# Side work of a fused attention kernel issued two parts at a time in every second quarter, and the products with the values one quarter earlier

## The chip, the cores and the metric

The kernel runs on one NeuronCore of a Trainium2 chip. The metric is the time of one execution on the device, in microseconds (us). The engines are named as in the profile: PE is TensorE (matmuls; PEld is its weight loads), DVE is VectorE, ACT is ScalarE, POOL is GpSimd, SP only issues transfers. Each engine works through its own list of instructions in order and waits at semaphores for the others.

## The reference

Eight batches of 1024 tokens and 256 channels go through four layers, each adding to x:

```python
x = x + attn_a(layernorm(x))   # one distance matrix for all 16 heads, causal softmax of -|p_i - p_j|/4
x = x + ffn(layernorm(x))      # r * (relu(xk W_k)^2 W_v), with xr, xk mixed from x and the token before
x = x + attn_b(layernorm(x))   # 16 heads of width 16, causal softmax, no output projection
x = x + ffn(layernorm(x))      # the same weights again
# attn_b, per batch and head:
scores = einsum('bhqd,bhkd->bhqk', q, k) / 4, causal
out    = einsum('bhqk,bhkd->bhqd', softmax(scores), v)
```

Everything is in float32; the queries and keys of attn_b are split into three bfloat16 parts each, so that one bfloat16 matmul with 96 rows gives the float32 scores.

## The kernel before

**The backbone.** attn_b sets the rhythm. Its work is cut into groups of 4 heads (4 groups for a batch, 32 in all), a group into 12 pieces, and a piece into 4 quarters, one for each head. Quarters are numbered u from 0 to 1535, then a few more to finish; quarters with negative numbers hold the work before attn_b can start. In this text q0 to q3 are the first to fourth quarter of a piece. In a quarter PE issues one matmul of the scores for the row maxima (L922, out `max_bank`, two buffers; it waits until DVE has reduced the one of two quarters before, L989 on the diagonal and L992 off it) and, 14 pieces behind it, one matmul of the transposed scores for the exponentials (L935, out `exp_bank`, two buffers; it waits for ACT's exponential L973 of two fills before). Key pieces narrower than 512 columns put 2 or 4 heads into one bank, and ACT then works only at the last of them. Once in a piece, after the two matmuls of q3, PE multiplies the exponentials of the piece before with the values: four float32 matmuls into `o_bank`, one for each head in a column group of its own (L954; the text calls these four "the products"). They wait for the last exponential of that piece, on the diagonal also for POOL's causal selection (L1011), and at the first piece of each half of the queries for ACT's copy of `o_bank` (L1059), which empties it from the half before and stands in ACT's list at q1 of the same piece.

**Side jobs.** All else on PE (the other three layers, the projections of attn_b, transposes) is cut into parts of some 0.4 to 0.9 us that are issued between the quarters. They write three `side` banks. `JOBS` and `stage_jobs` give each job the quarter in which its first part is due, its number of parts, the step between them and the delay after which another engine empties the bank. `place()` walks over the quarters and gives each quarter at most one part: the list is sorted by due time, the first of it is taken when it is due and, for a job's first part, when a bank is free. A part that comes late sets `shift`, which moves what the other engines have of that stage (through `WRITTEN_AT` and `clock`) by as many quarters; it is regained by one quarter in four. `maxima` (two transposes that carry the maxima of a group to a row, L1032) and `output` (L1066) are no parts: they are placed by themselves, `maxima` at q1 and `output` at q2, and come ahead of the parts of their quarter.

**Order.** `schedule` writes every engine's list with the same loop over the quarters: first the quarter's attention, then what is due of maxima, output and the stages. The job names that matter below: `tr` (transposes of the normalised x, L442, emptied by ACT L432), `values1` (values of attn_a, L615, needs both L432 copies), `keys` (L741, needs DVE's L675), `attend` (L633, needs ACT's L560 and POOL's L578), `project` and `values3` (L825, L841, for attn_b), `receptance` and `products` (L755, of the ffn).

A batch of attn_b is a turn of 192 quarters. By `place()` a steady turn holds 122 parts: 42 in its first 96 quarters and 80 in its last 96.

Of the kernel before, what the change touches and what calls it, by code (L numbers as in the profile page):

```python
# [18 lines left out]
GH = 4  # L19
# [32 lines left out]
def exp_before(e):  # L52

    return EXP_PER_GROUP * (e // len(PACK)) + sum(GH // heads for heads in PACK[:e % len(PACK)])
# [9 lines left out]
PIECES = B * NS  # L64
# [65 lines left out]
def stage_jobs(s, n, h):  # L130
    jobs = [((name, s, n, h, k), *when) for name, k, *when in JOBS["ln"]]
    body = "ffn" if s in ("ffn2", "ffn4") else s
    if body == "ffn" or h == 0:
        late = apart("att1", n) - APART["att1"]
        if s == "att1":
            work = [("values1", t, 16 + t + (TPH + late) * (t // TPH), 1, 1, 2) for t in range(NT)] + \
                [("positions", k, 29 + k + late * (k // 3), 1, 1, 1) for k in range(6)] + JOBS["attend"]
        else:
            work = JOBS.get(body) or [("project", j, project_at(n, j), 2, 1, 1) for j in range(8)] + \
            [("values3", j, project_at(n, 2 * j) + 2, 2, 3, 2) for j in range(4)]  # L140
        jobs += [((name, s, n, h, k), *when) for name, k, *when in work]
    return jobs


def place():

    parts, delay = [], {}
    for start, s, n, h in STAGES:
        for key, first, count, step, after in stage_jobs(s, n, h):
            delay[key] = after  # L150
            parts += [(start + first + step * k, key, k, k == count - 1) for k in range(count)]
    parts.sort(key=lambda part: part[0])
    rows = [(4 * NP * (g + 1) + 1, ("maxima", g)) for g in range(GROUPS)]
    rows += [(OUTPUT_AT[h] + 4 * NP * g + 5, ("output", g, h)) for g in range(GROUPS) for h in range(2)]
    rows += [(at, ("setup", k)) for k, at in enumerate(SETUP_AT)]
    rows.sort()
    quarters, bank, emptied, late = {}, {}, {}, []
    free, before, shift, u = [BEGIN, BEGIN, BEGIN], BEGIN, 0, BEGIN
    while parts or rows:
        while rows and rows[0][0] <= u and min(free) <= u:  # L160
            key = rows.pop(0)[1]
            k = free.index(min(free))
            quarters[key], bank[key], emptied[key] = [u], k, u + 2
            free[k] = u + 2
        if parts:
            at, key, k, last = parts[0]
            regained = max(0, shift - max(0, at - before) // 4)
            if at + regained <= u and (k > 0 or min(free) <= u):
                parts.pop(0)
                before, shift = at, max(regained, u - at)  # L170
                late.append((at, shift))
                if k == 0:
                    bank[key] = free.index(min(free))
                    free[bank[key]] = NEVER
                    quarters[key] = []
                quarters[key].append(u)
                if last:
                    emptied[key] = free[bank[key]] = u + delay[key]
        u += 1
    return quarters, bank, emptied, late  # L180


NEVER = 10 ** 6
BEGIN = STAGES[0][0]
PARTS_AT, BANK, EMPTIED_AT, LATE = place()
END = max(EMPTIED_AT.values()) + 20


WRITTEN_AT = {}
for k in range(BEGIN, END):  # L190
    since, shift = ([(BEGIN, 0)] + [entry for entry in LATE if entry[0] <= k])[-1]
# [11 lines left out]
def bass_hybrid(nc, x, wq, bq, wk, bk, wv, bv, wo, bo, w3d, b3d, wkqv, bkqv, w_r, w_k, w_v,  # L203
# [7 lines left out]
    with ExitStack() as ctx:  # L211
        def sb(name, shape, dt=F32):
            return ctx.enter_context(nc.sbuf_tensor(name, shape, dt))
# [37 lines left out]
        shift = sb("shift", [P, 2, TPH])  # L251
# [17 lines left out]
        parts = sb("parts", [P, 2, 3, HALF], BF16)  # L269
# [625 lines left out]
        emptied = [None, None, None]  # L895
# [14 lines left out]
        def pe_att3(u):  # L910
            pe = nc.tensor
            t, j = divmod(u, GH)
            e = t - LEAD
            if 0 <= t < PIECES:
                g, m = divmod(t, NP)
                if m == 0 and j == 0:
                    pe.wait_ge(stack_ready[g % STACKS], 16 * N_STACK_DMA * (g // STACKS + 1))
                tile, k0, k1 = QUERY_PIECES[m]
                r = g % STACKS
                if u >= MAX_BANKS:  # L920
                    pe.wait_ge(max_free, u + 1 - MAX_BANKS)
                pe.matmul(max_bank[u % MAX_BANKS][:, 0:k1 - k0], qs[r][0:KROWS, j, P * tile:P * (tile + 1)],  # L922
                          ks[r][0:KROWS, j, k0:k1], start=True, stop=True).then_inc(max_full, 1)
            if 0 <= e < PIECES:
                g, m = divmod(e, NP)
                if m == 0 and j == 0:
                    if g == 0:
                        pe.wait_ge(rows_of_ones, STACKS)
                    pe.wait_ge(crow_ready, 32 * (g + 1))
                kt, q0, q1 = KEY_PIECES[m]  # L930
                r = g % STACKS
                k, slot = exp_before(e) + j // PACK[m], j % PACK[m]
                if k >= EXP_BANKS and slot == 0:
                    pe.wait_ge(exp_done, k + 1 - EXP_BANKS)
                mm = pe.matmul(exp_bank[k % EXP_BANKS][:, (q1 - q0) * slot:(q1 - q0) * (slot + 1)],  # L935
                               ks[r][:, j, P * kt:P * (kt + 1)], qs[r][:, j, q0:q1], start=True, stop=True)
                if slot == PACK[m] - 1:
                    mm.then_inc(s_full, 1)
            if j == GH - 1 and 1 <= e <= PIECES:
                g, m = divmod(e - 1, NP)  # L940
                n = g // NG
                kt, q0, q1 = KEY_PIECES[m]
                h = 0 if m < TPH else 1
                if g == 0 and m == 0:
                    pe.wait_ge(consts_ready, 8)
                if g % NG == 0 and m == 0:
                    pe.wait_ge(v3_ready, 4 * n + 4)
                pe.wait_ge(exp_done, exp_before(e))
                if DIAGONAL[m]:
                    pe.wait_ge(sel_done, NT * g + NTH_DIAGONAL[m] + 1)  # L950
                if kt == 0:
                    pe.wait_ge(ot_ready, 2 * g + h)
                for j in range(GH):
                    mm = pe.matmul(o_bank[32 * j:32 * j + VW, q0 - HALF * h:q1 - HALF * h],  # L954
                                   v3[n % 2][:, kt, GH * (g % NG) + j, :], pt[:, (e - 1) % 2, j, 0:q1 - q0],
                                   start=(kt == 0), stop=(q1 - q0 == P), skip_group_check=True)
                mm.then_inc(pv_done, 1)
# [342 lines left out]
        @block.tensor  # L1300
        def _(pe):
            pe.wait_ge(consts_ready, 2)
            def stage(at, s, n, h):
                body = {"att1": [pe_att1(n), pe_positions(n)], "proj3": [pe_proj3(n), pe_values3(n)]}.get(s, []) if h == 0 else []
                return [pe_transposed(s, n, h)] + ([pe_ffn(s, n, h)] if s in ("ffn2", "ffn4") else body)

            schedule([pe_setup()], pe_att3, pe_maxima, pe_output, stage)
# [27 lines left out]
```

## Time and profile before

| | us |
|---|---|
| median of 3 runs | 2104.41 (2093.51 to 2106.41) |
| the profiled execution: its time | 2109.85 |
| its span, first to last instruction | 2108.1 |

| engine | busy us | share |
|---|---|---|
| PE | 1849.2 | 88% |
| DVE | 1467.0 | 70% |
| ACT | 1323.7 | 63% |
| POOL | 728.2 | 35% |

The mean granted clock of PE is 0.943 of full speed. A matmul's duration in the profile overlaps that of the next, so the time that a matmul really takes from PE is read from its start to the next one's start.

### The profile page before, as it was taken

How to read it: one execution, taken by the hardware profiler on the slowest of the kernel's cores; microseconds unless marked ns; L12 is line 12 of the kernel's file. 1: busy time of each engine (PE TensorE's matmuls, PEld its weight loads, DVE VectorE, ACT ScalarE, POOL GpSimd, SP SyncE). 2: the span in 40 equal slices, each digit the busy share in tenths (PEclk: the TensorE clock that was granted, in tenths of full speed). 3: DMA queues.
4: the chain of work that ended last, by engine and by line, in shares of the span. 5: the costliest groups of instructions: out<-in, count | busy, mean ns of one | idle time of the engine just before them, and what ended most of it. 6: DMA issues, size and time to landing. Idle time of an engine off the chain costs nothing. (4 is left out here: it accounts for less than half of the span.)

```text
span 2108.1 us, 32379 instructions
## 1 busy us (share of the span) xinstructions
PE 1849.2 (88%) x9842; PEld 922.5 (44%) x9842; DVE 1467.0 (70%) x4288; ACT 1323.7 (63%) x2585; POOL 728.2 (35%) x879
## 2 busy tenths in 40 slices
PE   5677898889997999889998899979998899988986
PEld 4453443335543455434543355434544345322423
DVE  5576778767676677667786667766776677768642
ACT  3564355876569565776758665695657766455664
POOL 1342332234333253333443243333532334312313
PEclk8797899999998999999999899989999999989998
DMA  3006113111131112410132111311124101322000
GB/s 85 1 23 123 26 56 67 31 31 32 55 76 31 31 31 82 80 21 12 41 110 42 31 31 56 76 31 31 34 83 76 22 11 41 99 33 50 13 21 20
DMA packets 64346, 97.26 MB, mean 46 GB/s; under 512 B 15655, under 2 KB 58029, under 8 KB 58030
## 3 DMA queue, kind: packets, MB, share of 16 engines
q1 hardware_dynamic: 64174, 95.20, 20.2%
q8 instruction: 80, 1.31, 0.3%
q14 instruction: 92, 0.75, 0.1%
HBM read 61.09 MB, written 33.55 MB: 45 GB/s over the span
## 5 line engine op out<-in xcount | busy, mean ns | idle before, releaser
L973 ACT ACTIVATE pt<-exp_bank 128x512 f32<-128x512 f32 (+1 forms) x1216 | 698.9, 582 | 526.6 <-PE exp_bank L935 521.0
L989 DVE CUSTOM_DVE_ANT_0 max_bank<-max_bank,mask 128x128 f32<-128x128 f32 (+3 forms) x1024 | 501.8, 500 | 400.9 <-PE max_bank L922 386.4
L922 PE MATMUL max_bank<-ks,qs 96*128 96x512 bf16 (+3 forms) x1536 | 523.5, 346 | 85.9 <-DVE piece_max L992 44.9
L935 PE MATMUL exp_bank<-qs,ks 98*128 98x512 bf16 (+3 forms) x1536 | 515.4, 342 | 40.0 <-ACT pt L973 37.0
L992 DVE TENSOR_REDUCE piece_max<-max_bank 128x1 f32<-128x512 f32 x512 | 344.1, 686 | 94.4 <-PE max_bank L922 90.2
L954 PE MATMUL o_bank<-pt,v 128*17 128x512 f32 (+3 forms) x3072 | 334.1, 508 | 13.7 <-POOL pt L1011 11.0
L922 PEld LDWEIGHTS max_bank<-ks,qs 96*128 96x128 bf16 x1536 | 150.9, 99 | 399.5 <-DVE piece_max L989 140.9
L1011 POOL TENSOR_SCALAR_AFFINE_SELECT pt<-pt 128x512 f32<-128x512 f32 x256 | 171.5, 670 | 412.6 <-ACT pt L973 411.8
L935 PEld LDWEIGHTS exp_bank<-qs,ks 98*128 98x128 bf16 x1536 | 152.4, 100 | 236.0 <-ACT pt L973 118.5
L633 PE MATMUL side<-vp,p 128*128 128x260 f32 x576 | 171.4, 423 | 28.7 <-ACT p L560 21.0
L412 ACT ACTIVATE xh<-xs,shift,rstd 128x256 f32<-128x256 f32 x256 | 149.7, 596 | 47.8 <-POOL shift L401 47.8
L589 POOL TENSOR_TENSOR sq<-sq 128x512 f32<-128x512 f32 (+1 forms) x96 | 97.3, 1013 | 226.3 <-ACT sq L536 226.3
L536 ACT ACTIVATE sq<-pb,neg_pos 128x512 f32<-128x512 f32 (+3 forms) x264 | 167.0, 633 | 3.6 <-ACT p L560 0.4
L741 PE MATMUL side<-pb,wkT 128*128 128x512 f32 x240 | 139.3, 669 | 9.3 <-DVE pb L675 9.2
L989 DVE DVE_READ_ACCUMULATOR2_ANT piece_max<- 128x1 f32 x1024 | 144.5, 141 | 0.3
L633 PEld LDWEIGHTS side<-vp,p 128*128 128x128 f32 x576 | 111.2, 207 | 74.1 <-issue 31.1
L825 PE MATMUL side<-xt,wkq 128*128 128x512 f32 x256 | 136.8, 619 | 3.0 <-ACT xt L432 1.5
L755 PE MATMUL side<-wrT,pb 128*128 128x256 f32 x480 | 126.3, 387 | 0.0
L755 PE MATMUL side<-wvT,pb 128*128 128x256 f32 x480 | 125.7, 386 | 0.0
L1090 POOL TENSOR_TENSOR xs<-xs,on 128x256 f32<-128x256 f32 x64 | 49.3, 770 | 208.5 <-DVE on L1080 208.4
L664 POOL TENSOR_TENSOR xs<-xs,tm 128x512 f32<-128x512 f32 x64 | 98.3, 1541 | 66.2 <-DVE tm L692 66.2
L791 POOL TENSOR_TENSOR parts<-x,parts 128x512 bf16<-128x512 f32 x64 | 74.9, 1170 | 108.3 <-DVE parts L775 108.3
(119 smaller groups left out, 2348.4 us busy)
## 6 DMA issues: line engine op xcount, KB each, us to landing
parts_dram<-parts SPq DMA_DIRECT2D x64, 384.0 KB, 2.6
qs<-parts_dram SPq DMA_DIRECT2D x192, 128.0 KB, 7.2
ks<-parts_dram SPq DMA_DIRECT2D x32, 384.0 KB, 4.7
xs<-in_L_attn_a_x_dram SPq DMA_DIRECT2D x16, 512.0 KB, 4.2
ks<-parts_dram SPq DMA_DIRECT2D x32, 256.0 KB, 5.4
out_dram<-xs SPq DMA_DIRECT2D x16, 512.0 KB, 3.1
ks<-parts_dram SPq DMA_DIRECT2D x32, 128.0 KB, 5.8
qs<-neg_maxT SPq DMA_DIRECT2D x64, 8.0 KB, 1.9
```

The source lines that it names most:

```text
L412: act.activation(xh[:, t, :], src[:, TPH * h + t, :], ACT.Identity, bias=shift[:, r, t:t + 1], scale=rstd[:, r, t:t + 1]).then_inc(xh_read ...
L536: mm = act.activation(sq[:, p % 2, c, 0:w], pb[:, c, q0:q1], ACT.Square, bias=neg_pos[:, kt, c:c + 1])
L633: mm = pe.matmul(bank[:, 0:VC], p1[:, at:at + P], vp[:, kt, :], start=(kt == 0), stop=(kt == t))
L741: mm = pe.matmul(bank[:, :], wkT[:, c, P * j:P * (j + 1)], xk[:, c, :], start=(c == 0), stop=(c == NC - 1))
L755: mm = pe.matmul(bank[:, C * t:C * (t + 1)], lhs[:, c, P * (2 * j + t):P * (2 * j + t + 1)], rhs[:, c, :], start=(c == 0), stop=(c == NC - 1))
L922: pe.matmul(max_bank[u % MAX_BANKS][:, 0:k1 - k0], qs[r][0:KROWS, j, P * tile:P * (tile + 1)], ks[r][0:KROWS, j, k0:k1], start=True, stop= ...
L935: mm = pe.matmul(exp_bank[k % EXP_BANKS][:, (q1 - q0) * slot:(q1 - q0) * (slot + 1)], ks[r][:, j, P * kt:P * (kt + 1)], qs[r][:, j, q0:q1] ...
L954: mm = pe.matmul(o_bank[32 * j:32 * j + VW, q0 - HALF * h:q1 - HALF * h], v3[n % 2][:, kt, GH * (g % NG) + j, :], pt[:, (e - 1) % 2, j, 0: ...
L973: act.activation(pt[:, e % 2, j + 1 - heads:j + 1, 0:w], exp_bank[k % EXP_BANKS][:, 0:heads * w].rearrange("p (j n) -> p j n", j=heads), A ...
L989: dve.tensor_tensor_reduce(scores, scores, mask[:, HALF - w:HALF], 1.0, LOWEST, ALU.add, ALU.max, piece_max[:, j, m:m + 1]).then_inc(max_f ...
L992: dve.tensor_reduce(piece_max[:, j, m:m + 1], scores, AX.X, ALU.max).then_inc(max_free, 1)
L1011: pool.affine_select(out=block, in_=block, compare_op=ALU.is_ge, fill=0.0, base=0, pattern=[[0, GH], [1, P]], channel_multiplier=-1).then_ ...
```

## The change

`place()` gives a quarter with u of 0 or more no part when u is even and up to two when u is odd. In exchange a part may be taken ahead of its due time: a job's first part by one quarter, its other parts by two. Below u = 0 all stays as it was. The products with the values are issued at q2 instead of q3, with the same waits. Nothing is added to or taken from what is computed; `maxima`, `output`, L1059 and the selections keep their places.

```diff
-        if parts:
+
+        for _ in range(1 if u < 0 else 2 * (u % 2)):
+            if not parts:
+                break
             at, key, k, last = parts[0]
             regained = max(0, shift - max(0, at - before) // 4)
-            if at + regained <= u and (k > 0 or min(free) <= u):
-                parts.pop(0)
-                before, shift = at, max(regained, u - at)
-                ...
+            if at + regained > u + (u >= 0) * (1 if k == 0 else 2) or k == 0 and min(free) > u:
+                break
+            parts.pop(0)
+            before, shift = at, max(regained, u - at)
+            ...
...
-            if j == GH - 1 and 1 <= e <= PIECES:
+            if j == GH - 2 and 1 <= e <= PIECES:
                 g, m = divmod(e - 1, NP)
```

## Rows read from the trace of the kernel before

**Rows 1.** The page, part 1: an engine's busy time, share, instructions.
```profile
PE 1849.2 (88%) x9842; PEld 922.5 (44%) x9842; DVE 1467.0 (70%) x4288; ACT 1323.7 (63%) x2585; POOL 728.2 (35%) x879
```
**Rows 2.** Stretches: length, busy us and instructions of each engine, granted clock, DMA.
```profile
1125.20:1242.00 116.80, 101.84 (x553) 47.04 (x550) 80.78 (x245) 86.14 (x177) 41.66 (x56) 0.93 0.16 28
1242.00:1371.00 129.00, 123.29 (x680) 66.25 (x678) 96.38 (x285) 78.78 (x151) 49.00 (x53) 1.00 0.28 67
...
1137.00:1151.00 14.00, 11.34 (x74) 5.22 (x75) 11.95 (x30) 12.16 (x26) 5.80 (x7) 1.00 0.41 59
1151.00:1171.00 20.00, 15.58 (x81) 4.01 (x73) 12.32 (x35) 19.29 (x38) 5.39 (x6) 0.91 0.00 1
...
1206.00:1214.00 8.00, 7.39 (x29) 1.99 (x28) 7.07 (x17) 4.45 (x8) 1.82 (x3) 0.57 0.00 0
1214.00:1242.00 28.00, 28.00 (x147) 14.70 (x146) 18.14 (x56) 19.84 (x39) 12.23 (x13) 1.00 0.00 1
```
**Rows 3.** Timeline of PE, 80-part half: start, duration, line, tiles, idle before.
```profile
1007.72 0.33 PE L922 MATMUL max_bank<-ks,qs 96*128 96x384 bf16 x1
1007.88 0.38 PE L935 MATMUL exp_bank<-qs,ks 98*128 98x512 bf16 x1
1008.10 1.03 PE L755 MATMUL side<-wvT,pb 128*128 128x256 f32 x4
1008.96 0.33 PE L922 MATMUL max_bank<-ks,qs 96*128 96x384 bf16 x1
```
**Rows 4.** Waits of PE, whole span: us in total, times, longest.
```profile
PE max_bank L922 <- DVE piece_max L992: 44.9, 80, 1.4
PE exp_bank L935 <- ACT pt L973: 37.0, 90, 0.6
PE max_bank L922 <- DVE piece_max L989: 35.1, 89, 1.3
...
PE side L633 <- ACT p L560: 21.0, 11, 8.1
PE o_bank L954 <- POOL pt L1011: 11.0, 16, 1.2
...
PE side L1032 <- DVE neg_max L1001: 8.5, 14, 0.8
```
**Rows 5.** Timeline around a copy of o_bank, where ACT is full.
```profile
1157.80 0.62 ACT L1059 ACTIVATE ot<-o_bank 128x512 f32<-128x512 f32 x1
...
1157.98 0.39 PE L935 MATMUL exp_bank<-qs,ks 98*128 98x512 bf16 x1 [0.49 <-ACT pt L973]
```
**Rows 6.** Timeline around a maxima job, 80-part half.
```profile
1304.77 0.38 PE L922 MATMUL max_bank<-ks,qs 96*128 96x512 bf16 x1
...
1305.25 1.05 PE L954 MATMUL o_bank<-pt,v 128*17 128x512 f32 x8
1306.23 1.12 PE L825 MATMUL side<-xt,wkq 128*128 128x512 f32 x2
...
1308.49 0.28 PE L1032 MATMUL side<-identb,neg_max 128*32 128x128 bf16 x2
```
**Rows 7.** Timeline around the first values1, 80-part half.
```profile
1339.79 0.39 PE L922 MATMUL max_bank<-ks,qs 96*128 96x512 bf16 x1
1339.82 0.59 ACT L432 ACTIVATE xt<-side 128x512 f32<-128x512 f32 x1
...
1340.46 1.14 PE L615 MATMUL side<-wvp,xt 128*128 128x259 f32 x4
```
**Rows 8.** Timeline around the first keys of a layer.
```profile
1209.05 0.74 DVE L675 SCALAR_TENSOR_TENSOR pb<-pb,cols,xt 128x512 f32<-128x512 f32 x1
...
1209.19 0.61 PE L922 MATMUL max_bank<-ks,qs 96*128 96x512 bf16 x1 [0.23 <-DVE piece_max L992]
```
**Rows 9.** Timeline: the first attend of a batch.
```profile
1130.35 0.68 PE L633 MATMUL side<-vp,p 128*128 128x260 f32 x2 [1.30 <-ACT p L560]
```
**Rows 10.** Waits of PE in the 80-part half, 1242 to 1371 us.
```profile
PE side L600 <- DVE on L1080: 0.8, 1, 0.8
PE side L841 <- ACT xt L432: 0.8, 1, 0.8
PE side L1032 <- DVE neg_max L1001: 0.8, 1, 0.8
PE side L442 <- ACT x L784: 0.6, 1, 0.6
```

More of the change, by code:

```diff
@@ L164, in place @@
             free[k] = u + 2
-        if parts:
+        for _ in range(1 if u < 0 else 2 * (u % 2)):
+            if not parts:
+                break
             at, key, k, last = parts[0]
             regained = max(0, shift - max(0, at - before) // 4)
-            if at + regained <= u and (k > 0 or min(free) <= u):
-                parts.pop(0)
-                before, shift = at, max(regained, u - at)
[L171 to L178, printed above, removed]
+            if at + regained > u + (u >= 0) * (1 if k == 0 else 2) or k == 0 and min(free) > u:
+                break
+            parts.pop(0)
+            before, shift = at, max(regained, u - at)
+            late.append((at, shift))
+            if k == 0:
+                bank[key] = free.index(min(free))
+                free[bank[key]] = NEVER
+                quarters[key] = []
+            quarters[key].append(u)
+            if last:
+                emptied[key] = free[bank[key]] = u + delay[key]
         u += 1
```

## Prediction

> **What bounds the kernel now.** I first read the engines' shares: PE is busy 88% of the span, the next, DVE, 70% [rows 1]. A share is a mean over unlike stages, so I read stretches next. Steady turns repeat, and I take the one from 1125.2 to 1371 us. Its half with 80 parts takes 129.0 us with PE busy 123.29; the half with 42 takes 116.8 with PE busy 101.84 [rows 2]. Inside the first kind PE has no gap at all (28.00 of 28.00 us from 1214 on); inside the second ACT alone is full for 20 us (19.29), and before it DVE and ACT share the blame (11.95 and 12.16 of 14) [rows 2]. So the bound alternates.
>
> The timeline of a full quarter shows what PE is made of: 0.16 us for 384 columns of maxima, 0.22 for 512 of exponentials, 0.86 for a part, each start following the last at once [rows 3]. The product of 512 columns takes 0.98 (1305.25 to 1306.23) [rows 6]. Going over from one kind to another costs nothing, so **doing two parts in a row saves PE no time by itself**: a gain can only be a wait that goes.
>
> The waits of PE say how much there is: 44.9 + 35.1 us for DVE to free a maxima bank, 37.0 for ACT to free an exponentials bank, 21.0 at attend, 11.0 at products for a selection, 8.5 at maxima [rows 4]. These are understated: a 512-column record lasts 0.38 us where its successor can start after 0.22, so each of the 259 bank waits hides 0.16 more. Bank waits are thus 117 + 41 = 158 us.
>
> **Evenness.** With 512-column banks and parts of 0.86 everywhere, q0 to q3 take 1.30, 1.30, 1.30 and 2.28 us before, and 0.44, 2.16, 1.42 and 2.16 after; the piece takes 6.18 both times. A bank wait depends on the time over two quarters, since banks are reused after two. Before, these windows are 2.60, 2.60, 3.58, 3.58; after, 2.60, 3.58, 3.58, 2.60: the same four, rotated. So where PE is full I expect no bank wait to come or go. Where no parts are, moving the products only rotates the piece. A gain needs pieces with a few parts, half bound by PE in q3 and by DVE in q0 to q2; there the longest quarter (products and part) is split.
>
> **The parts, by hand from the rule.** Due times in the ffn stages come in even-odd pairs (keys at 842 and 843, then 844 and 845). After, both parts of a pair go into the odd quarter before (841, 843). Attends likewise (784, 785 into 783). The projections of a turn, which now slip until the next stage is 4 quarters late, fit without lateness: values1, due at 932, goes from 936 to 933, and attn_a behind it starts 4 quarters sooner. Parts issued per turn stay 122. Five terms follow, then the sum.
>
> 1. **Products one quarter sooner: +14 us.** Of the 384, the 63 behind a copy of `o_bank` are the tight ones. The copy stands at q1; it starts 0.2 us before the last scores matmul of q3 in a full ACT, and lasts 0.62 [rows 5]. At q2 PE comes after 0.44 us of matmuls, where ACT needs an exponential and the copy, about 0.6 + 0.6 less overlap: some 0.5 us too early, 32 us for 63. Where two parts stand in q1 they cover it (1.72), and where ACT or DVE is full PE would have waited at the next bank anyway. Selections on the diagonal already cost 11.0 [rows 4]; one quarter less slack at narrow pieces adds a few more. Bounds 0 and 38; I take 14, as two thirds lie in the stretches bound by ACT or DVE.
>
> 2. **Maxima: +8.** L1032 needs DVE's reduction of the last scores of the group, issued in q3 (1304.77), and is reached at q1, 3.6 us later, with the 0.98 of the products between [rows 6]. After, the products stand ahead of that q3, so PE arrives up to 0.98 sooner at a place where it already waits. 31 x 0.98 = 30 is the upper bound, 0 the lower (all absorbed by DVE, which works on meanwhile). Worked through group by group with the parts in between it is 15; half of the groups are in DVE-bound stretches: 8.
>
> 3. **Parts pulled ahead: +19.** Tight ones per turn: values1 starts 0.05 us after ACT's second L432 ends (1340.41), and one quarter earlier PE would be there at 1339.79: 0.7 us of waiting, twice [rows 7]; by the new plan L432 and values1 even share a quarter. Keys: L675 ends at 1209.79, PE would be there at 1209.19: 0.7 [rows 8]. With small ones about 3 us a turn, in stretches where PE is the bound, so nothing hides it: 6.5 turns give 19. Bounds 0 and 30. The ffn's products and receptance have over 4 us of slack and cost nothing.
>
> 4. **Less lateness: -25.** The first attend waits 1.30 us [rows 9], the second about as much, because regaining `shift` squeezes the chain from squares to selection; without lateness each has a quarter more. Of 21.0 us [rows 4], 8.1 of it ahead of u = 0, I take 13 as gained. ACT's squares start 4 quarters sooner, out of the ACT-full stretch and into one where ACT is busy 78.78 of 129 [rows 2]: 1 us a turn, 6. Waits for `side` banks and the like (0.8 each [rows 10]) are dealt anew; a quarter of some 4 us a turn, 6. Bounds 0 and 50.
>
> 5. **Bank waits in mixed pieces: -22.** Of the 158 us most lie in stretches where ACT or DVE is full, which no order mends. Limiting each piece with parts to what DVE and ACT both had idle leaves 44 us. I take half; bounds 0 and 60.
>
> Sum: 14 + 8 + 19 - 25 - 22 = -6 us on the profiled execution's 2109.85, so 2104. The median lies 5.4 below that execution, so I say 2098. A measurement of this kernel can tell about 1% from no change.
>
> **A clock rule.** Around 1206 to 1214 the granted clock is 0.57 of full, so most of it is at 1.2 GHz; the stretch from 1214 on, full of work, has 1.00, that is 2.4 GHz [rows 2]. Ahead of 1206 PE had kept waiting for DVE. The Trainium skill ("TensorE: Matmul & The Clock Gate", Part 1) says the throttled state is the default and sustained activity lifts it. By that rule, new waits that thin out PE's work could start a further slow stretch; the trace agrees that slow stretches follow waiting. This is rival D.
>
> **Rivals.**
> A, likeliest (0.40): gains and costs nearly cancel, 2098; own range 2078 to 2130.
> B (0.32): smoothing works better. Terms 4 and 5 near their far ends (-50, -45) against costs of 41 give 54 less: 2050. For it: the bank waits are the largest item [rows 4] and the bound alternates within pieces. Against: windows over two quarters are the same four, and ACT is full in 20 us of each turn.
> C (0.18), the other side: the cover of the pulled parts and the products is gone. Costs 30 + 20 + 28 against 38 of gain give +40: 2145. It decides if values1, keys and the first products of each half wait over 0.7 us each in the 80-part half. For it: they start within 0.1 us of their inputs now [rows 7, 8].
> D (0.10): the clock. The half with 42 parts has a mean of 0.93 [rows 2], so 16 us of it at half speed. As much again would cost 8 us a turn, some 48 in all: 2146. Less of it would gain as much.
>
> **How the numbers follow.** Faster by over 1% (below 2083): B 0.32 and 0.03 of A and D: 0.35. Slower by over 1% (above 2125): C 0.16, D 0.07, 0.03 of A: 0.26. Between: 0.39. B ends at 2050 and C at 2145; 2052 to 2140 leaves out about 2 in 10.
>
> **What the profile after would show.** Right: bank waits (117 in rows 4) near 90, attends (21.0) near 12, products waiting 20 to 30 instead of 13.6, L1032 near 15 instead of 8.5, values1 and keys together near 15; the 80-part half 128 to 131 us, the other 112 to 117. B: the 42-part half below 112. C: the 80-part half above 132 with waits at L615, L741 and L954. D: granted clock away from 0.943. The forecast fails if bank waits rise in the 80-part half (windows misjudged), or if pairing makes `side` banks short.

## The result, and the profile after

The change makes the kernel **slower by 9.1%**: 2294.28 us (median of 4 runs, 2287.51 to 2301.20) against 2104.41 for the kernel before (median of 3 runs; a fourth one, 2414.66 us, was disturbed and is left out), ratio 1.0911 [1.0860, 1.0963]. The ratios here and below are estimates from repeated runs with a 95% interval, and can differ a little from a quotient of two medians. The profiled execution took 2301.20 us with a span of 2299.4, so 191.3 us more than the span of before. The four lines that the diff adds to `place()` move every later line of the kernel by 4: L922 of before is L926 here, L442 is L446, L741 is L745, L954 is L958.

The shares of the kernel after, the page's part 1:

```profile
PE 1929.3 (84%) x9842; PEld 934.0 (41%) x9842; DVE 1477.4 (64%) x4288; ACT 1328.3 (58%) x2585; POOL 712.3 (31%) x879
```

Beside [rows 1] the counts are the same and DVE, ACT and POOL are busy nearly as long. PE is busy 80 us longer with the same matmuls, and idle 111 us longer. The first points to its clock: the mean granted clock fell from 0.943 to 0.907. The traces record only two levels, full and half (2.4 and 1.2 GHz), so (1 - clock) x 2 x span is the time at the lower one: 240 us before, 428 after.

The same steady turn as in [rows 2] (stretch, length, busy us and instructions of each engine, granted clock, DMA):

```profile
1220.40:1346.00 125.60, 105.55 (x550) 47.14 (x548) 81.03 (x244) 85.15 (x175) 40.31 (x54) 0.89 0.15 26
1346.00:1490.00 144.00, 127.32 (x678) 66.99 (x677) 97.20 (x283) 80.62 (x153) 48.05 (x54) 0.96 0.24 60
```

The half with 42 parts went from 116.8 us to 125.6, the half with 80 from 129.0 to 144.0. The half in which PE had been almost gapless lost most, and its clock is no longer full throughout (0.96).

The waits of PE over the span (total us, times, longest), to be read against [rows 4]:

```profile
PE side L446 <- ACT xh L416: 61.9, 44, 9.7
PE max_bank L926 <- DVE piece_max L996: 38.1, 86, 1.3
PE side L745 <- DVE pb L679: 37.8, 29, 3.6
PE max_bank L926 <- DVE piece_max L993: 37.5, 100, 1.3
PE exp_bank L939 <- ACT pt L977: 28.9, 64, 0.9
PE side L1036 <- DVE neg_max L1005: 25.9, 25, 1.6
PE o_bank L958 <- ACT ot L1063: 18.9, 31, 1.1
PE o_bank L958 <- POOL pt L1015: 17.4, 20, 1.7
PE side L637 <- ACT p L564: 12.8, 3, 8.1
PE side L619 <- ACT xt L436: 11.5, 7, 1.8
```

The same lines of before that [rows 4] did not need:

```profile
PE side L442 <- ACT xh L412: 22.8, 7, 9.7
...
PE side L741 <- DVE pb L675: 9.2, 3, 3.6
...
PE side L615 <- ACT xt L432: 2.6, 6, 0.8
PE o_bank L954 <- ACT ot L1059: 2.6, 14, 0.2
```

Two jobs that hardly waited before, the transposes of the normalised x and the keys, now head the list: 7 waits became 44, and 3 became 29.

**Where the 191 us went.** Records of matmuls overlap and hide short waits, so PE's whole timeline is taken from start to start, and what each step costs at full clock is subtracted (0.22 us for 512 bfloat16 columns, 0.86 for a part, as in [rows 3]). In the stretches that the trace records at the lower level the same columns take twice as long: all 110 steps of the trace of before that lie within a side part and wholly in such a stretch take about twice their time at full clock, or more. So for a step in such a stretch its cost at full clock is counted once more, as the price of the clock. What is left stands at the line ahead of which it falls. The work at full clock is 1600 us in both kernels (and in every variant below but one). The rest, in us:

| beyond the work | before | after | difference | products one quarter earlier alone | pairs alone |
|---|---|---|---|---|---|
| lower clock | 89.7 | 162.8 | +73.1 | 158.8 | 92.4 |
| `tr` (L442) | 36.9 | 81.5 | +44.6 | 41.5 | 83.6 |
| `keys` (L741) | 21.4 | 53.8 | +32.4 | 21.1 | 56.1 |
| the products (L954) | 52.1 | 78.3 | +26.2 | 105.1 | 52.4 |
| `maxima` (L1032) | 12.4 | 30.6 | +18.2 | 28.2 | 17.8 |
| `values1` (L615) | 13.8 | 25.7 | +11.9 | 22.4 | 25.1 |
| scores for the maxima (L922) | 126.9 | 132.0 | +5.1 | 131.9 | 130.5 |
| L825, L600, L841 together | 26.4 | 30.0 | +3.6 | 26.1 | 30.5 |
| scores for the exponentials (L935) | 62.5 | 52.6 | -9.9 | 39.1 | 65.5 |
| `attend` (L633) | 36.9 | 26.2 | -10.7 | 35.8 | 33.4 |

These differences add up to +194.5 and the lines not listed to -3.1, so nothing of the 191.3 is missing. The last two columns are kernels of the first experiments. The lower clock is the largest single item. A rough check needs no account: in the stretches at the lower level PE is busy 191.8 of 244.3 us before and 360.4 of 431.6 after, and about half of that busy time is what the lower level adds. Of the +73.1 us, 69 stand in steps that no idle time of PE follows, so they are not hidden in a wait. In the fourteen traces of this case a microsecond at the lower level costs 0.34 to 0.38 us; below I take 0.37. At the banks the listed waits fall from 117.0 us to 104.5, and by this account, which counts hidden ones too, L922 and L935 together go from 189.4 to 184.6: no real change.

### The profile page after: what moved, and what is told of

Read it like the earlier page. It is cut to its first block and busy times, and to the rows that moved or that the text cites. A ratio compares the mean times of both kernels' runs of the same rounds, so it can differ in the third digit from the quotient of the medians.

```text
span 2299.4 us, 32379 instructions
## 1 busy us (share of the span) xinstructions
PE 1929.3 (84%) x9842; PEld 934.0 (41%) x9842; DVE 1477.4 (64%) x4288; ACT 1328.3 (58%) x2585; POOL 712.3 (31%) x879
## 3 DMA queue, kind: packets, MB, share of 16 engines
q1 hardware_dynamic: 64174, 95.20, 18.4%
## 5 line engine op out<-in xcount | busy, mean ns | idle before, releaser
L977 ACT ACTIVATE pt<-exp_bank 128x512 f32<-128x512 f32 (+1 forms) x1216 | 689.9, 577 | 678.6 <-PE exp_bank L939 676.6
L926 PE MATMUL max_bank<-ks,qs 96*128 96x512 bf16 (+3 forms) x1536 | 538.2, 356 | 82.6 <-DVE piece_max L996 38.1
L939 PE MATMUL exp_bank<-qs,ks 98*128 98x512 bf16 (+3 forms) x1536 | 535.9, 356 | 32.8 <-ACT pt L977 28.9
L958 PE MATMUL o_bank<-pt,v 128*17 128x512 f32 (+3 forms) x3072 | 357.5, 540 | 36.7 <-ACT ot L1063 18.9
L926 PEld LDWEIGHTS max_bank<-ks,qs 96*128 96x128 bf16 x1536 | 153.7, 100 | 491.8 <-DVE piece_max L993 207.0
L637 PE MATMUL side<-vp,p 128*128 128x260 f32 x576 | 159.5, 414 | 20.7 <-ACT p L564 12.8
L745 PE MATMUL side<-pb,wkT 128*128 128x512 f32 x240 | 143.4, 730 | 37.9 <-DVE pb L679 37.8
L446 PE MATMUL side<-ident,xh 128*128 128x128 f32 x512 | 82.1, 287 | 69.3 <-ACT xh L416 61.9
L637 PEld LDWEIGHTS side<-vp,p 128*128 128x128 f32 x576 | 113.3, 205 | 51.9 <-issue 18.2
L958 PEld LDWEIGHTS o_bank<-pt,v 128*17 128x17 f32 x3072 | 54.1, 97 | 169.4 <-issue 106.6
L759 PE MATMUL side<-wvT,pb 128*128 128x256 f32 x480 | 114.5, 382 | 0.0
L759 PE MATMUL side<-wrT,pb 128*128 128x256 f32 x480 | 113.9, 380 | 0.0
```

The costliest lines, as they stand in the source:

```text
L637: mm = pe.matmul(bank[:, 0:VC], p1[:, at:at + P], vp[:, kt, :], start=(kt == 0), stop=(kt == t))
L745: mm = pe.matmul(bank[:, :], wkT[:, c, P * j:P * (j + 1)], xk[:, c, :], start=(c == 0), stop=(c == NC - 1))
L759: mm = pe.matmul(bank[:, C * t:C * (t + 1)], lhs[:, c, P * (2 * j + t):P * (2 * j + t + 1)], rhs[:, c, :], start=(c == 0), stop=(c == NC - 1))
L977: act.activation(pt[:, e % 2, j + 1 - heads:j + 1, 0:w], exp_bank[k % EXP_BANKS][:, 0:heads * w].rearrange("p (j n) -> p j n", j=heads), A ...
```

## The experiments

Twelve kernels ran, each beside runs of the kernel before on its own chip. That kernel's median differs by chip (2107.79 for the first four, 2088.36 for the next four, 2093.14 for the last four), so kernels of different groups are compared by their ratios, not by their microseconds. "Time at the lower clock" is (1 - clock) x 2 x span. It too differs by chip for the kernel before (240, 196 and 205 us), so the last column gives what a kernel has above the before of its own chip, medians of runs; the column ahead of it is the profiled execution. Lines of a kernel that carries the new `place()` have the numbers of the kernel after (in shifted and repaired one more), of others those of before.

| kernel | ratio to before | lower clock, us | above before, us |
|---|---|---|---|
| pv_only | 1.0579 [1.0528, 1.0630] | 435 | +173 |
| pairs_only | 1.0515 [1.0483, 1.0547] | 257 | +10 |
| ahead_only | 1.0132 [1.0103, 1.0162] | 247 | +1 |
| tight_later | 1.0638 [1.0596, 1.0680] | 399 | +152 |
| pairs_even | 1.0249 [1.0215, 1.0283] | 273 | +84 |
| two_due | 1.0023 [1.0003, 1.0044] | 193 | -3 |
| pv_copy | 1.0526 [1.0487, 1.0565] | 352 | +151 |
| pv_busy | 1.0791 [1.0750, 1.0832] | 271 | +67 |
| shifted | 1.0697 [1.0654, 1.0741] | 385 | +182 |
| repaired | 1.0466 [1.0429, 1.0504] | 328 | +134 |
| pv_fixed | 1.0416 [1.0379, 1.0454] | 331 | +120 |
| maxima_q2 | 1.0053 [1.0028, 1.0077] | 214 | +30 |

### One half of the change at a time

**pv_only**: the kernel before with only the products moved.

```diff
-            if j == GH - 1 and 1 <= e <= PIECES:
+            if j == GH - 2 and 1 <= e <= PIECES:
```

> The kernel before with only the products moved from q3 to q2 (parts one a quarter, as before). Theory S (side parts lost the time they had behind their inputs): little changes at the side jobs; the waits at the products (13.6 us before, 36 after) and at maxima (8.5 before, 25.9 after) rise as in the whole change, so 2105 + 25 = about 2130, and granted clock near 0.94. Theory P (the products moved ahead are the cause): most of the 189 us is here, over 2230. Theory G (it balances the quarter, as the forecast had it): 2085 to 2105.

**pairs_only**: the kernel after with the products back at q3 (`j == GH - 1`).

> The kernel before with only the new placing of the parts (two by two in odd quarters, ahead of their due time), the products still at q3. Theory S: most of the loss, 2105 + 150 = about 2250, with PE waiting over 50 us at the transposes L446 for ACT and over 30 at keys L745 for DVE, as in the whole change. Odd quarters at q3 now hold products and two parts, so q3 is the longest quarter by far; bank waits at q1 and q2 rise a little. Theory P: within 1% of before. The two kernels pv_only and pairs_only should then add up to about the whole, +189.

Measured: 2234.18 and 2215.43 us beside 2107.79. Each half is slow by itself, and 5.8% + 5.2% is more than the 9.1% of both; that the products alone would cost 25 us was wrong. They are slow in different ways. The two waits in pairs_only:

```profile
PE side L446 <- ACT xh L416: 62.3, 45, 9.7
...
PE side L745 <- DVE pb L679: 37.6, 29, 3.6
```

So these two waits come from the pairs alone, to within half a microsecond. In pv_only:

```profile
PE max_bank L922 <- DVE piece_max L992: 39.7, 84, 1.4
PE o_bank L954 <- POOL pt L1011: 37.0, 27, 2.1
PE max_bank L922 <- DVE piece_max L989: 35.3, 99, 1.3
PE o_bank L954 <- ACT ot L1059: 24.0, 42, 1.1
PE side L1032 <- DVE neg_max L1001: 23.5, 26, 1.6
```

The products wait 61.0 us where they waited 13.6 (11.0 and 2.6), `maxima` 23.5 instead of 8.5, the waits for a maxima bank, the next on the way, hardly shrink (80.0 to 75.0), and the lower clock holds for 435 us instead of 240: 69 of the 132 us by the table above. The halves of the steady turn in pv_only show where:

```profile
1181.70:1306.60 124.90, 107.92 (x550) 48.63 (x548) 80.82 (x245) 86.55 (x177) 40.76 (x55) 0.86 0.15 26
1306.60:1441.40 134.80, 122.98 (x679) 65.98 (x677) 97.10 (x282) 79.18 (x151) 49.80 (x54) 1.00 0.26 64
```

The half with few parts has a clock of 0.86 instead of 0.93 and 8.1 us more; the other keeps its clock and has 5.8 us more, all of it waits.

### Pulling ahead or pairing?

The pairs do two things: parts are taken ahead of their due time, and even quarters are left empty. **ahead_only** does the first alone, one part a quarter as before; **two_due** allows two in a quarter but none ahead, which takes the lateness away and leaves the rest; **pairs_even** puts the pairs into the even quarters. All have the products at q3.

```diff
 # ahead_only
-        for _ in range(1 if u < 0 else 2 * (u % 2)):
+        for _ in range(1):
 # two_due
-        for _ in range(1 if u < 0 else 2 * (u % 2)):
+        for _ in range(1 if u < 0 else 2):
-            if at + regained > u + (u >= 0) * (1 if k == 0 else 2) or k == 0 and min(free) > u:
+            if at + regained > u + 0 or k == 0 and min(free) > u:
 # pairs_even
-        for _ in range(1 if u < 0 else 2 * (u % 2)):
+        for _ in range(1 if u < 0 else 2 * (1 - u % 2)):
```

> The kernel before, one part in every quarter and the products at q3, but a part may be taken ahead of its due time as in the change (first part by one quarter, others by two). Separates the pulling ahead from the empty even quarters. If the pulling ahead alone costs (a part reaches its input one quarter sooner), the transposes, keys and values1 wait as in the whole change and it takes over 2180. If it is the empty even quarter between input and part (0.44 us instead of 1.3) that takes the slack, this one loses only what the forecast's third term said, some 20 to 40 us: 2125 to 2145.

> The kernel before, but a quarter may take two parts when both are due, none ahead of its time; no part is late any more in the steady turns. Tests the gain from less lateness that the forecast's fourth term took (25 us for the whole change). By that term 2105 - 20 = about 2085; if lateness cost nothing, 2105; if values1 and keys then wait for inputs because the time was needed, 2110 to 2120.

> The mirror of the change: two parts in every even quarter (q0, q2), none in odd ones, with the same pulling ahead, and the products at q3 as before. The balance over the quarters is that of the change, but the tight parts (transposes, keys, values1), all due in even quarters, stand where they are due, and a loaded quarter lies between their input and them. Theory S (the parts lost the time behind their inputs): waits at L446 and L745 go back to 38 and 10 to 25 us and the products wait as before, so 2095 to 2130. Theory E (two parts in one quarter cost in themselves, whatever they wait for): it stays near pairs_only, 2190 to 2230.

Pulling ahead costs 1.3%, some 28 us. The other three quarters of the pairs' 5.2% come with the empty even quarters. In ahead_only the keys already wait as often as in the kernel after, the transposes much less:

```profile
PE side L446 <- ACT xh L416: 29.9, 14, 9.7
PE side L745 <- DVE pb L679: 29.6, 30, 3.6
```

With the pairs in the even quarters both waits are nearly those of before, though just as many quarters are empty:

```profile
PE max_bank L926 <- DVE piece_max L993: 51.4, 128, 1.3
PE max_bank L926 <- DVE piece_max L996: 48.4, 83, 1.8
...
PE side L446 <- ACT xh L416: 24.6, 8, 9.7
...
PE side L745 <- DVE pb L679: 11.1, 10, 3.6
```

So the pairing and the empty quarters by themselves don't make them wait. By `place()` the first transposes of one stage, for example, stand at quarter 830 before, at 829 in the kernel after and at 830 in pairs_even; the first keys at 842, 841 and 842. In the even phase nothing that is due in an even quarter is pulled ahead. The long waits need both: a part that is pulled by one quarter (ahead_only: 14 waits of `tr`) and an empty quarter ahead of it (44). What pairs_even still loses (2.5%, some 52 us) is to a good half the lower clock: it holds for 84 us more than in the before of the same chip, by estimate 31 us of time (84 x 0.37). The rest stands at the bank waits, 127.6 us for the three instead of 117.0, and in many small ones. two_due is no faster than before (1.0023), although the attends' 21.0 us are down to 12.2: **taking the lateness away alone is worth nothing that can be measured.**

### Are the two waits the cause?

**tight_later** gives the two jobs their quarter back: due one quarter later in the kernel after. They are then due in odd quarters and are not pulled: by `place()` the first transposes stand at 831 (830 before, 829 after), the first keys at 843 (842 and 841). **shifted** begins every stage one quarter later, with the same effect on all jobs.

```diff
 # tight_later
-JOBS = {"ln": [("tr", c, 12 + c, 1, 1, 2) for c in range(NC)],
+JOBS = {"ln": [("tr", c, 13 + c, 1, 1, 2) for c in range(NC)],
-        "ffn": [("keys", j, 24 + 2 * j, 2, 1, 1) for j in range(2)] +
+        "ffn": [("keys", j, 25 + 2 * j, 2, 1, 1) for j in range(2)] +
 # shifted
+STAGES = [(start + (start >= 0), s, n, h) for start, s, n, h in STAGES]
```

> The whole change, but the transposes are due one quarter later and so are the keys, which by the rule of placing puts them two quarters later where they had been pulled ahead. Theory S: the waits at L446 (61.9 us) and at keys L745 (37.8) fall by more than half, and the time by 60 to 100 us, to about 2210. Theory C (the slow clock is the cause and not a consequence): the waits fall but cold time stays near 430 us and the time stays above 2260.

> The whole change with every side stage that starts at u = 0 or later begun one quarter later. Balance over the quarters as in the change (pairs in q1 and q3, products at q2), but the tight parts are now due in odd quarters and are no longer taken ahead, and their inputs' quarter is a loaded one. Theory S: waits at L446 (61.9) and L745 (37.8) return to about 23 and 17, the time to 2294 - 80 = about 2210, near pv_only (the waits at products, selections and maxima stay). Theory E (two parts in one quarter cost in themselves): it stays over 2270.

Both take the waits away, and the time follows in part: the ratio falls from 1.0911 to 1.0638 and 1.0697, some 57 and 45 us. In shifted the two waits are 22.7 us (7 times) and 8.2 (3 times), as before. In tight_later:

```profile
PE side L446 <- ACT xh L416: 19.4, 4, 9.7
...
PE side L745 <- DVE pb L679: 7.1, 3, 3.6
```

By the start-to-start account `tr` falls from 81.5 to 31.9 and `keys` from 53.8 to 8.4, 95 us in all. Later waits take back a part: L922 132.0 to 160.7, products 78.3 to 86.7, `values1` 25.7 to 32.3; the lower clock gives another 9 (162.8 to 153.5). A wait of PE taken away here is worth a little more than half its length. So the two waits are a cause of the loss, but hardly of the low clock: tight_later still has 152 us more of it than its before.

### What the products wait for

**pv_copy** is pv_only with ACT's copy of `o_bank` one quarter earlier as well (q0); to keep the order of the rest, `output` and the last ffn stage start stay where they were. **pv_fixed** has `maxima` one quarter later (q2) on top. **maxima_q2** is the kernel before with `maxima` at q2.

```diff
 # pv_copy, pv_fixed (against before, beside GH - 2)
-OUTPUT_AT = [4 * (LEAD + TPH + 1) + 1, 4 * (LEAD + NP + 1) + 1]
+OUTPUT_AT = [4 * (LEAD + TPH + 1), 4 * (LEAD + NP + 1)]
 # pv_fixed, maxima_q2
-    rows = [(4 * NP * (g + 1) + 1, ("maxima", g)) for g in range(GROUPS)]
+    rows = [(4 * NP * (g + 1) + 2, ("maxima", g)) for g in range(GROUPS)]
```

> pv_only (products at q2) with ACT's copy of o_bank one quarter earlier as well (q0 instead of q1), the output transposes staying at q2. If the products' loss comes from the copy standing one quarter ahead of them, the wait for L1059 (24 us in pv_only) vanishes and the time falls by 20 to 40 us, to about 2200; the waits for the selection (37 us) and at maxima (23.5) stay. If the copy only hides other waits, the time stays at 2230.

> pv_copy with maxima one quarter later (q2, behind the products). Expected: the 23 us that PE waits there go, 2198 - 20 = about 2175, that is +70 on before; the rest is the selection (36 us) and half clock (353 us of it). If the wait only moves on to the bank waits: no change.

> The kernel before with nothing changed but maxima one quarter later (q2 instead of q1). PE waits 8.5 us at this place before, 14 times, and its DMA has quarters to spare; so 2105 - 5 to 10, a ratio of 0.995 to 1.0. If the DMA of the maxima row is late then, PE waits at L935 for qs<-neg_maxT instead.

In pv_only the wait for the copy looks like this (timeline: start, duration, engine, line, tiles, idle before):

```profile
1198.63 0.60 ACT L1059 ACTIVATE ot<-o_bank 128x512 f32<-128x512 f32 x1
...
1199.38 1.05 PE L954 MATMUL o_bank<-pt,v 128*17 128x512 f32 x8 [0.82 <-ACT ot L1059]
```

With the copy at q0 this wait goes from 24.0 us to 0.2. The ratio goes from 1.0579 to 1.0526; the two intervals overlap, so it isn't shown that the time fell at all. By the start-to-start account the products lose 27.6 us less (105.1 to 77.5) and the bank waits take 13.9 back (171.0 to 184.9). With `maxima` later too it is 1.0416, which is 1.1% below pv_copy and outside the intervals. The same move of `maxima` in the kernel before does nothing good (1.0053), although it clears L1032's 8.5 us: the lower clock holds for 30 us more than in the before of its chip, by estimate 11 us, which is the whole loss, and the waits of L935 for the DMA of the maxima row, named in the expectation, are 5.7 us instead of 0.8.

What pv_fixed keeps above before, 4.2%, has three parts that the profile shows: products waiting for selections, waits for a maxima bank (100.9 us instead of 80.0), and the clock, with 120 us more at the lower level by estimate 44 of the 87 us. The first:

```profile
PE o_bank L954 <- POOL pt L1011: 38.7, 33, 2.1
```

Its chain in pv_only, where it is longest:

```profile
1247.98 0.28 DVE L468 SCALAR_TENSOR_TENSOR sq<-sq 128x128 f32<-128x128 f32 x1
...
1248.30 0.31 ACT L550 ACTIVATE sq<-sq 128x128 f32<-128x128 f32 x1 [3.36 <-DVE sq L468]
1248.52 0.58 ACT L973 ACTIVATE pt<-exp_bank 128x512 f32<-128x512 f32 x1
...
1249.26 0.67 POOL L1011 TENSOR_SCALAR_AFFINE_SELECT pt<-pt 128x512 f32<-128x512 f32 x1 [3.86 <-ACT pt L973]
1250.07 0.63 PE L954 MATMUL o_bank<-pt,v 128*17 128x256 f32 x8 [2.06 <-POOL pt L1011]
```

The exponential that the selection needs stands in ACT's list behind an instruction of the other attention, L550, which waits 3.36 us for DVE. Its counterpart before has the same chain, of which the products at q3 hid one quarter:

```profile
1189.36 0.63 PE L954 MATMUL o_bank<-pt,v 128*17 128x256 f32 x8 [0.97 <-POOL pt L1011]
```

0.97 us became 2.06: at such narrow pieces a quarter is one part and two short matmuls, 1.1 us, and all of it is lost.

### What the clock does

**pv_busy** asks whether the low clock is a cause or only an effect. It is pv_only with the scores for the maxima issued twice (into the same bank, same values) in the 680 quarters that have no part, so that PE is busier where it is thin; 117 us of work more at full clock.

```diff
+IDLE = set(range(PIECES * 4)) - {u for at in PARTS_AT.values() for u in at}
-                pe.matmul(max_bank[...], ..., start=True, stop=True).then_inc(max_full, 1)
+                for _ in range(2 if u in IDLE else 1):
+                    mm = pe.matmul(max_bank[...], ..., start=True, stop=True)
+                mm.then_inc(max_full, 1)
```

> pv_only with the scores matmul of the maxima issued twice in the 680 quarters that hold no side part (the same result into the same bank), which keeps PE busier where it would wait. Theory C (slow clock is a cause of its own): time at half clock falls from 435 us to under 250 and the kernel gets faster, 2234 - 30 = about 2200, although 680 x 0.2 = 136 us of work is added. Theory W (the clock only follows the waits and costs little): the time stays or rises by 20 to 80 us.

Measured: 1.0791 against pv_only's 1.0579, so 117 us of work cost 2.1%, some 45 us. Above the before of its own chip the lower clock holds for 67 us instead of pv_only's 173, by estimate 39 us of time; the rest of the added work, some 30 us, went into waits that were there anyway (all items of the account but the clock: 470.8 to 427.8 us). So the clock falls because PE's work is thinner, and it costs time of its own; but filling up does not pay for itself. The time came out as theory W had it, the clock more as theory C.

### A version with all repairs

**repaired** is the kernel after with every stage one quarter later (shifted), the copy at q0 and `maxima` at q2.

> shifted, with the copy of o_bank a quarter earlier (q0, output transposes still at q2) and maxima a quarter later (q2). If the loss is the sum of the slacks taken (parts behind inputs, copy, maxima), what is left over is the selection wait and the clock: 2150 to 2170. If a part of the loss is none of these, it stays above 2190.

It takes 2191.91 us beside 2093.14, 1.0466: half of the loss is back, but it isn't faster than before, so by the expectation's own sign a part of the loss is none of the slacks named. Its steady turn and its waits:

```profile
1162.30:1288.00 125.70, 106.01 (x548) 48.36 (x547) 82.17 (x245) 87.63 (x179) 41.34 (x55) 0.89 0.15 26
1288.00:1418.00 130.00, 121.27 (x680) 65.95 (x678) 95.87 (x282) 77.51 (x149) 47.90 (x53) 1.00 0.26 66
```

```profile
PE max_bank L927 <- DVE piece_max L994: 63.4, 123, 2.3
PE max_bank L927 <- DVE piece_max L997: 57.6, 120, 1.7
```

The 80-part half is almost that of before (130.0 against 129.0) with a full clock. The 42-part half stays at 125.7 us against 116.8, and the waits for a maxima bank are 121.0 us instead of 80.0. The lower clock holds for 134 us more than in the before of the same chip, by estimate 50 of the 98 us that are left. Why the banks are the worse for products at q2 and paired parts in pieces with few of them, while DVE has 35% of that half to spare, is not known; no run tells it apart.

No kernel of the study beats the one before.

## Why the prediction was wrong

The forecast was -6 us on the profiled execution, the result +191. Set against the start-to-start table the miss of 197 us divides among its steps so (the lines not listed take 3 back):

| step | said | measured, in the whole change | missed |
|---|---|---|---|
| 3, parts pulled ahead | +19 | +44.6 +32.4 +11.9, and 12.3 at L825 and L600: +101.2 | 82 |
| clock (rival D, not in the sum) | 0 | +73.1 | 73 |
| 5, bank waits | -22 | +5.1 -9.9: -4.8 | 17 |
| 1, products | +14 | +26.2 | 12 |
| 2, maxima | +8 | +18.2 | 10 |
| 4, less lateness | -25 | -10.7 at attends, -8.7 at L841: -19.4 | 6 |

Two steps failed above all: term 3, and the clock, which the sum put at nothing.

**Term 3 failed in its kind, not only in its size.** It took the timeline of before and asked when PE would be there one quarter sooner. But in that timeline the even quarter before a consumer holds a part of its own; in the new order it holds none. Look at the transposes, before:

```profile
1216.22 0.60 ACT L412 ACTIVATE xh<-xs,shift,rstd 128x256 f32<-128x256 f32 x1
1216.29 1.02 PE L741 MATMUL side<-pb,wkT 128*128 128x512 f32 x2
...
1217.37 0.38 PE L935 MATMUL exp_bank<-qs,ks 98*128 98x512 bf16 x1
1217.59 0.60 PE L442 MATMUL side<-ident,xh 128*128 128x128 f32 x4
```

and after:

```profile
1316.91 0.38 PE L926 MATMUL max_bank<-ks,qs 96*128 96x512 bf16 x1
1317.13 0.38 PE L939 MATMUL exp_bank<-qs,ks 98*128 98x512 bf16 x1
...
1318.14 0.60 ACT L416 ACTIVATE xh<-xs,shift,rstd 128x256 f32<-128x256 f32 x1
...
1318.79 0.65 PE L446 MATMUL side<-ident,xh 128*128 128x128 f32 x4 [1.28 <-ACT xh L416]
```

Before, ACT is done at 1216.82 and PE arrives at 1217.59, a slack of 0.77 us that a look at waits alone doesn't show. After, PE is free at 1317.35 and starts at 1318.79: 1.44 us of waiting. The slack fell by 0.77 + 1.44 = 2.21 us, which is a quarter pulled, 1.30, and the part that is gone from the even quarter, 0.86. By the first alone it would wait 0.53, and the prediction did not even list this job among the tight ones. pairs_even and tight_later show the cause: where the parts aren't pulled, by the other phase or by due times one later, 44 and 29 waits are 8 and 10, or 4 and 3. The price that term 3 put on pulling alone was near in size, 19 said, 28 measured by ahead_only, but not in its make-up: the keys alone rise by 27 us there (21.4 to 48.7), the rest nearly cancels.

For the keys the prediction had the place and the row [rows 8] but 0.7 us each (the row gives 0.60); in the kernel after, the first keys of a layer wait longer, and their two parts (x4) then run at the lower clock, 3.78 us where the next two take 1.88 at full clock:

```profile
1308.93 0.74 DVE L679 SCALAR_TENSOR_TENSOR pb<-pb,cols,xt 128x512 f32<-128x512 f32 x1
1309.73 3.78 PE L745 MATMUL side<-pb,wkT 128*128 128x512 f32 x4 [0.89 <-DVE pb L679]
...
1314.76 1.88 PE L745 MATMUL side<-pb,wkT 128*128 128x512 f32 x4
```

**Evenness, and term 5.** The sums over two quarters are indeed the same four, rotated, and in pairs_only bank waits hardly change (+3.6 and +3.0 us at the two lines). But the sums say nothing of inputs, which cross a single quarter, and they are 0.44 us for an empty one. Of the gain of 22 us the change shows 5. pv_only has 18 (189.4 to 171.0), but there new waits at the products come ahead of the banks; in repaired, where most of those are gone, the bank waits are 57 us longer than before (246.5), though nothing is added to DVE or ACT. The 158 us that the prediction took for all of them was low too: hidden ones included they are 189.4. What is measured here is the size; why the mixed pieces gave no gain, and why repaired loses, is open.

**Term 1 and the absorption.** The half microsecond by which the products come before the copy was about right: 42 waits, 24.0 us in pv_only, against 63 x 0.5 = 32 at most. The step that failed is "a few more" for selections (11.0 became 37.0) and "two thirds are absorbed": alone, the products lose 53.0 us (52.1 to 105.1) and the bank waits give back 18.4, a third. Also `maxima`, +15.8 alone where 8 was said, near the 15 that the prediction had worked out before halving it.

**The clock.** Rival D had a chance of 0.10 and a price of 48 us; it came with the waits, not instead of them: 73 us in the change, 69 in pv_only. It had the place right only in part: the half with few parts goes from 0.93 to 0.89, the other from 1.00 to 0.96. The Trainium skill ("TensorE: Matmul & The Clock Gate", Part 1) says that the throttled state is the default and activity releases it; the traces agree, since the same work with longer waits runs 428 instead of 240 us at the lower level, and 117 us of added work lift it again. The step that failed was to treat the clock as a case of its own instead of a surcharge on every new wait.

**Term 4** was right as a wait (attends 21.0 to 12.8 us, "near 12" was said) but two_due shows that, taken alone, it is worth nothing in the end.

Of the list of signs, those of "right" failed but for the attends: bank waits 104.5 (near 90 said), products 36.3 (20 to 30), L1032 25.9 (near 15), `values1` and `keys` 49.3 (near 15), halves of 144.0 and 125.6 us (128 to 131, 112 to 117). Rival D's sign came true, 0.907 instead of 0.943, and rival C's in part: the 80-part half is above 132 (144.0), and in it L619 and L745 wait, 3.1 and 2.8 us, but the products don't; they wait in the other half (3.3). Bank waits in the 80-part half rose from 0.5 to 1.8 us, a sign of failure by the prediction's own list, though not where the time went. Rival C had the mechanism, "the cover of the pulled parts and the products is gone"; it was priced at +40 because it too counted only values1, keys and the products, and no clock.

## What to carry to other kernels

Where an order is planned in slots, write the slack of each dependency in time, as what stands between producer and consumer, and do it again in the new order: emptying a slot shortens every dependency that crosses it, also those that show no wait today. A regular pattern (every second slot) pulls all jobs of one phase alike, so try the other phase early. And a new wait on the bounding engine isn't absorbed by a later one where it also lets the engine's clock fall: taking 95 us of waits away gave back 57, while the new waits at four matmuls in each piece cost 5.8%, about half of it by the clock. Price the lower clock with every wait, not as a case of its own.

## What the runs showed of the hardware

- Moving four matmuls in each piece by one quarter, with all work unchanged, took the time at 1.2 GHz from 240 to 435 us in the profiled executions (240 to 413 in medians of runs). It's the half where PE waits often but briefly that slows: 0.93 to 0.86, while the other half stays at 1.00.
- A microsecond at the lower level cost this kernel and its variants 0.34 to 0.38 us of time, with PE busy for some 80% of such stretches (191.8 of 244.3 us before, 360.4 of 431.6 after).
- A `keys` pair takes 3.78 us at the lower level and 1.88 at the full one, so where the clock is low during a long part the engines behind it stand still too: DVE's next reduction waited 2.81 us for PE, ACT's next exponential 4.11.
- Changing between kinds of matmul costs PE nothing measurable, with one exception: ahead of the products, whose four heads have a column group each, about 0.09 us pass, the same in all kernels.
- One kernel's medians on different chips lie up to 0.9% apart (2088.36 to 2107.79), so microseconds of different chips can't be subtracted. By estimate most of it is the clock: 44 us more at the lower level (196 and 240) times 0.37 is 16 of the 19 us.
